# Down products over eight PSUM banks at once, with the second cross attention issued between them

## The reference, cut to what matters

```python
h  = silu(x @ Wgate.T) * (x @ Wup.T)           # 1792 hidden, weights dequantised, with LoRA
x  = layernorm(x + h @ Wdown.T)                # first down stage, then "x2"
s  = x @ (Wq.T @ Wk) @ ctx.T + beta            # second cross attention, per sequence of 128
x  = layernorm(x + softmax(s / sqrt(512)) @ ctx)   # "x3"
h  = silu(x @ G.T * gs) * (x @ U.T * us)       # ternary weights with a scale per row
x  = layernorm(x + (h @ Dn.T) * ds)            # second down stage, the output
```

## Time and profile before

| | us |
|---|---|
| median of 3 runs (721.57 to 722.71) | 722.56 |
| the profiled execution's own time | 721.29 |
| its span in the trace | 719.5 |
| PE busy | 668.8 (93%) |
| DVE busy | 404.9 (56%) |
| ACT busy | 379.6 (53%) |
| POOL busy | 66.9 (9%) |

### The profile page before, as it was taken

How to read it: one execution, slowest core, us unless ns; L and a number is a source line. 1 busy time by engine, 2 the same in 40 slices (tenths; PEclk the granted TensorE clock), 3 DMA queues, 4 the chain that set the end, 5 groups by cost and what they waited for, 6 DMA issues and landing times.

```text
span 719.5 us, 8570 instructions
## 1 busy us (share of the span) xinstructions
PE 668.8 (93%) x3228; PEld 468.4 (65%) x3228; DVE 404.9 (56%) x694; ACT 379.6 (53%) x536; POOL 66.9 (9%) x126
## 2 busy tenths in 40 slices
PE   5789999999998789999999999999997999999992
PEld 3544454545544348787877788888665888887872
DVE  3367768768558786474746434457677222223486
ACT  4456678965556418666666413444335333335653
POOL 1022213201111000000000000001121000000022
PEclk9979999999999899999999999999999999999997
DMA  5682086423223212242423000012641222210002
GB/s 156 204 288 91 2 267 195 153 79 103 70 62 95 89 33 92 63 124 63 123 64 96 1 0 1 0 35 85 246 149 30 61 86 60 88 31 0 1 29 89
DMA packets 24503, 62.97 MB, mean 88 GB/s; under 512 B 5477, under 2 KB 9637, under 8 KB 23566
## 3 DMA queue, kind: packets, MB, share of 16 engines
q1 hardware_dynamic: 24462, 62.43, 27.2%
HBM read 57.68 MB, written 4.73 MB: 87 GB/s over the span
## 4 chain that ended last, share of the span: by engine, by line
PE 81%; DVE 8%; ACT 4%; issue 2%; DMA 2%; POOL 1%; SPq 1%; POOLq 0%; DVEq 0%; ACTq 0%
PE bank L877 16%; PE bank L862 7%; PE bank L864 7%; PE bank L863 7%; PE bank L946 7%; PE bank L947 7%; PE bank L730 4%; PE bank L660 4%; PE bank L510 2%; PE bank L771 2%; PE bank L826 2%; PE bank L758 2%; PE bank L610 2%; PE bank L575 1%; PE bank L586 1%
## 5 line engine op out<-in xcount | busy, mean ns | idle before, releaser
L999 ACT ACTIVATE line<-line 128x1024 f32<-128x1024 f32 x87 | 91.1, 1047 | 0.1
L877 PE MATMUL bank<-wh,xh 128*128 128x512 f32 x224 | 87.8, 392 | 2.0 <-DVE xl L1684 1.8
L946 PE MATMUL bank<-xh,wh 128*128 128x512 f32 x224 | 87.4, 390 | 1.5 <-issue 1.5
L862 PE MATMUL bank<-xh,wh 128*128 128x512 f32 x224 | 88.7, 396 | 0.0
L877 PE MATMUL bank<-wh,xl 128*128 128x512 f32 x224 | 87.4, 390 | 0.0
L864 PE MATMUL bank<-xh,wl 128*128 128x512 f32 x224 | 87.3, 390 | 0.0
L863 PE MATMUL bank<-xl,wh 128*128 128x512 f32 x224 | 87.2, 389 | 0.0
L947 PE MATMUL bank<-xl,wh 128*128 128x512 f32 x224 | 87.2, 389 | 0.0
L1337 POOL TENSOR_SCALAR rstd<-mv 128x1 f32<-128x1 f32 x45 | 20.1, 447 | 633.0 <-DVE mv L1698 467.6
L1227 ACT ACTIVATE xh<-arena 128x512 fp32r<-128x512 f32 x56 | 35.4, 632 | 68.0 <-PE bank L877 59.8
L1684 DVE TENSOR_TENSOR xl<-arena,xh 128x512 fp32r<-128x512 f32 x56 | 38.5, 688 | 52.5 <-ACT xh L1227 52.3
(11 more groups left out here) (175 smaller groups left out, 1176.4 us busy)
## 6 DMA issues: line engine op xcount, KB each, us to landing
codes<-in_c_gu SPq DMA_DIRECT2D x14, 512.0 KB, 4.7
scales<-in_s_gu SPq DMA_DIRECT2D x28, 256.0 KB, 3.9
codes<-in_t_gu SPq DMA_DIRECT2D x14, 512.0 KB, 3.7
codes<-in_c_dn SPq DMA_DIRECT2D x7, 512.0 KB, 4.9
scales<-in_s_dn SPq DMA_DIRECT2D x14, 256.0 KB, 3.9
fold<-in_t_dn SPq DMA_DIRECT2D x1, 3584.0 KB, 12.8
codes<-in_c_qkv SPq DMA_DIRECT2D x6, 512.0 KB, 4.5
arena<-in_xT SPq DMA_DIRECT2D x4, 512.0 KB, 5.0
```

The costliest lines, as they stand in the source:

```text
L862: pe.matmul(dst, wh[:, s, c:c + P], xh[:, k, cols], start=(k == 0), stop=False)
L877: last = pe.matmul(late_bank(b)[:, :], h[:, s, b * P:(b + 1) * P], wp[:, s, 0:D], start=first and p == 0, stop=last_one and p == len(parts ...
L946: pe.matmul(dst, wh[:, s, c:c + P], xh[:, k, cols], start=(k == 0), stop=False)
L999: nc.scalar.activation(below(slot), below(slot), ACT.Prelu, bias=bias, scale=scale, alpha=alpha).then_inc(bent, 1)
```

## The change

Both down stages become one pass over all 8 blocks, with one bank for each block. Tiles 0 to 9 of the first stage (0 to 7 of the second) are walked tile by tile, all 8 blocks each. The last 4 tiles (6 in the second) are then walked block by block, so that blocks end one after another. A tile is prepared once, 1024 tokens wide, in four operand slots instead of two; the second stage puts its tiles 12 and 13 into two more, in the memory of `line` (`late_hidden`), with their weights in `wl`.

Between the block-wise products of the first stage stands the second cross attention: in step n PE issues block n's last 12 products in two groups of 6, with steps of blocks n-1, n-2 and n-3 around them. The x2 norm gets its own statistics tiles (`st2`, `mv2`, `rstd2`) and semaphores, ACT applies both norms (Identity with scale and bias), and DVE adds eps. POOL's stream alternates: the power for x2 of block n, then power and shift for x3 of block n-3. The third feed forward starts with group 0 of tiles 0 and 1 inside steps 8 and 9. The context is loaded when tile 13 has been split, the last down weights (`t_dn`) when its weight has been.

```diff
+TAIL = 3 * NT
+SLOTS = 4
+DN_LAST, T_LAST = NF - 4, NF - 6
...
+        def down_ready(j):
+            return j + 2
...
@@ sync
-                sp.wait_ge(dn_ready, NF + used)
+                sp.wait_ge(dn_low, down_ready(used - 1))
                 sp.dma_start(dst, src).then_inc(done, 16)
-            sp.wait_ge(d_ps, NT)
+            sp.wait_ge(dn_wlow, NF)
             sp.dma_start(t_dn, i["t_dn"]).then_inc(in_tdn, 16)
@@ tensor
+            def dn_group(j):
+                if j:
+                    dn_landed(j)
+                for b in range(NT):
...
+                    last = dn_products(j, b)
+                last.then_inc(hu_used, 1)
+            def dn_block(b, tiles, done=None):
+                for j in tiles:
+                    if b == 0:
+                        dn_landed(j)
+                    last = dn_products(j, b)
+                if done is not None:
                     last.then_inc(done, 1)
+            for j in range(DN_LAST):
+                dn_group(j)
...
+            half = DN_LAST + (NF - DN_LAST) // 2
+            for n in range(NT + 3):
+                if n < NT:
+                    dn_block(n, range(DN_LAST, half))
+                if 2 <= n < NT + 2:
+                    x_probT(n - 2)
+                if n < NT:
+                    dn_block(n, range(half, NF), d_ps)
+                if 1 <= n <= NT:
+                    x2_T(n - 1)
+                if 2 <= n < NT + 2:
+                    x_out(n - 2)
+                if 1 <= n <= NT:
+                    x_scores(n - 1)
+                if n >= 3:
+                    x3_T(n - 3)
+                if n >= NT:
+                    for q in range(n - NT, min(n - NT + 1, 2)):
+                        t_gu_pair(q, 0)
+            for j in range(2):
+                t_gu_pair(j, 1)
...
+            for j in range(T_LAST):
+                t_group(j)
+            for b in range(NT):
+                for j in range(T_LAST, NF):
+                    if b == 0:
+                        t_landed(j)
+                    last = t_products(j, b)
+                last.then_inc(t_d_ps, 1)
@@ scalar
+            for j in range(1, NF):
+                act.wait_ge(h_ready, TG * (j + 1) + 4)
+                if j >= SLOTS:
+                    act.wait_ge(hu_used, j - SLOTS + 1)
+                hidden_hi(hidden_part(xh, j), j, WHOLE, dn_hi)
+                dn_weight_hi(j)
...
+            for n in range(NT + 4):
+                if 2 <= n < NT + 2:
...
+                    nc.scalar.activation(probT[:, b % 2, :], late_bank(b)[:, P:2 * P], ACT.Copy).then_inc(xpT_ready, 1)
+                if 1 <= n <= NT:
+                    x_T_out(n - 1, late_index(n - 1), xT, x2_ps, x2_ready)
+                if n == NT:
+                    act.wait_ge(d_ps, NT)
+                    for s in range(2):
+                        t_gu_cast(s, 0, None)
+                if 3 <= n < NT + 3:
+                    norm_tail(3 * NT + n - 3)
+                if n < NT:
+                    x2_norm(n)
+                if 1 <= n <= NT:
...
+                    nc.scalar.activation(prob[:, b % 2, :], late_bank(b)[:, 0:P], ACT.Exp, bias=x_small(b, 0),
+                                         scale=float(D) ** -0.5, accum_out=x_small(b, 1)).then_inc(x_exp, 1)
+                if 3 <= n < NT + 3:
+                    x_T_out(4 * NT + n - 3, late_index(n - 3), xh)
...
+                if SLOTS <= j < NF - 2:
+                    act.wait_ge(t_used, j - SLOTS + 1)
+                hidden_hi(t_hidden_part(xh, j), j, WHOLE, t_dhi)
+                t_weight(j)
@@ gpsimd
+            def x2_rstd_of(b):
+                pool.wait_ge(x2_stats, b + 1)
+                nc.gpsimd.tensor_tensor(rstd2[:, b % 2, 1:2], rstd2[:, b % 2, 0:1], minus_half[:, :], ALU.pow).then_inc(x2_pow, 1)
+            for n in range(NT + 3):
+                if n < NT:
+                    x2_rstd_of(n)
+                if n >= 3:
+                    rstd_of(3 * NT + n - 3)
@@ vector
+            for n in range(NT + 4):
+                if n < NT:
+                    x2_stats_of(n)
+                if 1 <= n <= NT:
+                    x_max_of(n - 1)
+                if n < NT:
+                    x2_shift(n)
+                if 2 <= n < NT + 2:
+                    x_add(n - 2)
+                    stats_of(3 * NT + n - 2)
+                if 3 <= n < NT + 3:
+                    x_low(4 * NT + n - 3, (n - 3 + 2) % len(bank))
```

More of the change, by code:

```diff
@@ L869, in _ @@
                     gu_tile(s, 2 * n + s)
[L872 to L881, removed]
-                    last.then_inc(done, 1)
@@ L884, in down @@
[L884 to L894, removed]
@@ L896, in _, with down_products, dn_products @@
-            down((dn_ready,), ((xh, wh), (xh, wl), (xl, wh)), hu_used, d_ps, h_ready)
+            def down_products(b, hiddens, weights, first, last):
+                for p, (h, w) in enumerate(zip(hiddens, weights)):
+                    ins = pe.matmul(late_bank(b)[:, :], h[:, b * P:(b + 1) * P], w, start=first and p == 0, stop=last and p == len(hiddens) - 1)
+                return ins
+            def dn_products(j, b):
+                h, l, wh_j, wl_j = hidden_part(xh, j), hidden_part(xl, j), down_part(wh, j), down_part(wl, j)
+                return down_products(b, (h, h, l), (wh_j, wl_j, wh_j), j == 0, j == NF - 1)
@@ L935, in x3_T @@
[L935 to L946, removed]
-                    last = pe.matmul(dst, wh[:, s, c:c + P], xl[:, k, cols], start=False, stop=(k == KD - 1))
-                last.then_inc(done, 1)
@@ new lines, in _, with t_silu @@
+            silu_table()
+            def t_silu(j, tg):
+                s = j % 2
+                act.wait_ge(in_ts[s], 16 * (j // 2 + 1))
+                act.wait_ge(t_gate_ps, t_place(j, tg) + 1)
+                nc.scalar.activation(hT[:, j, tg * 512:(tg + 1) * 512], t_bank(j, tg, 0), ACT.Silu, scale=ff_s[:, s, 0:1]).then_inc(t_sil, 1)
+            for tg in range(TG):
+                for j in range(2):
+                    t_silu(j, tg)
+                    if tg:
+                        t_gu_cast(j, 1, 2 * (j + 1) + 1 - j)
@@ new lines, in _, with t_weight @@
+            for n in range(1, NF // 2 - 1):
+                for s in range(2):
+                    for tg in range(TG):
+                        t_silu(2 * n + s, tg)
+                    t_gu_cast(s, n + 1, 4 * n + 2 * s + 2)
+            def t_weight(j):
+                nc.scalar.activation(t_down_part(j), t_dn[:, j, :], ACT.Copy).then_inc(t_dw, 1)
+            for tg in range(TG):
+                t_silu(NF - 2, tg)
+            t_silu(NF - 1, 0)
+            act.wait_ge(in_tdn, 16)
+            act.wait_ge(t_up_ps, TG * NF - 1)
@@ L1314, in _ @@
+            for m in range(4 * NT, 5 * NT):
                 norm_tail(m)
@@ L1335, in rstd_of @@
                 pool.wait_ge(ln_stats, m + 1)
-                if m not in TURN:
+                if m < 3 * NT and m not in TURN:
                     link(nc.gpsimd.tensor_scalar(rstd[:, m % 2, 0:1], mv[:, m % 2, 1:2], LN_EPS, None, ALU.add))
@@ new lines, in t_hidden @@
+            def t_hidden(j, tg):
+                s = j % 2
+                dve.wait_ge(t_sil, t_place(j, tg) + 1)
+                dve.wait_ge(t_up_ps, t_place(j, tg) + 1)
+                h = hT[:, j, tg * 512:(tg + 1) * 512]
+                nc.vector.scalar_tensor_tensor(h, t_bank(j, tg, 1), ff_s[:, s, 1:2], h, ALU.mult, ALU.mult).then_inc(t_h, 1)
+            for tg in range(TG):
+                for j in range(2):
+                    t_hidden(j, tg)
+            for j in range(2, NF - 1):
+                for tg in range(TG):
+                    t_hidden(j, tg)
```

384 lines of the change are left out of this document (165 added, 219 removed).

## The result

The kernel after the change takes 729.16 us (median of 4 runs, 726.91 to 729.38) against 722.07 us for the kernel before (median of 4, 720.95 to 722.71). The ratio is 1.0093 [1.0068, 1.0117]: slower by 0.9%, with the direction as forecast and inside the range (720.5 to 731), but +7.1 us where +3.2 were forecast, and just above the 723.9 to 729 that the forecast itself covers.

What follows compares the result with a forecast made beforehand. PE's stream, busy 93%, was taken as the bound, only its waits and the tail as savable. Attention +7.9, second down stage +0.8 and tail -5.5 gave +3.2, added to the median: 725.8 us, range 720.5 to 731.

Steps and rivals of the forecast that it cites:

- The ring: Attention loop, steps 3 to 7: chain between blocks' last products through DVE, POOL, ACT, PE takes 7.96 us; PE waits 1.75, +8.8.
- the rival of slow powers: POOL's powers in the attention loop take 1.07 us each, adding 5 us, 731; chance 0.06.
- Start and end of the loop, tile 13: PE waits around the attention loop: 4.4 us at its start, 3.9 at its end, 1.1 for the first down stage's tile 13.
- The rival of smaller waits: Half of the 8.3 us of waits at the loop's start and end is gone: 721.8, no measurable change; chance 0.15.
- The table load: ACT's load ahead of the first exponential costs 1.28 us by the row, not the Trainium skill's 2.66.
- the granted clock: PE's clock in the attention, taken to stay at full speed, 2.4 GHz, at no cost.
- the drop: Rival: the clock falls to 1.2 GHz in the attention, doubling PE's part of five steps, +16, 742; chance 0.02.
- the attention's forecast: Attention beside the first down stage costs 46.1 us against 38.2, waits included: +7.9.
- Second down stage: Old waits go, new ones of 1.2, 1.0 and 1.0 us come at tiles 11 to 13: 54.8 us, +0.8.
- Tail: From PE's end to the span's end one block is left, not four: 7.35 us against 12.8, -5.5.
- Transfers: Context load takes 7.7 us with 5 us of cover; the down weights behind it may slow it; taken as nothing.
- Time against the median: The forecast's +3.2 was added to the median of runs, as the profiled execution's own time was 1.3 under it.

Runs made afterwards that it cites:

- POOL's order alone: The changed kernel with two calls swapped in POOL's loop, power and shift of x3's block n-3 ahead of x2's power: 718.95 us, ratio 0.9962 to the kernel before.
- both orders: The changed kernel with POOL taking x3's block before x2's, and the second down stage's tiles 12 and 13 prepared and used early: 714.39 us, ratio 0.9889.

## Why the prediction was right in direction and short in size

**The ring: right, a little too large.** Forecast were 7.96 us a step and a wait of 1.75, five times. The trace has 7.80 to 7.82 and a wait of 1.57. One pass around it, DVE, POOL and ACT in order of time, from the product that started at 521.13:

```profile
521.56 0.69 DVE L1821 TENSOR_TENSOR x<-x,bank 128x512 f32<-128x512 f32 x1 [1.37 <-PE bank L909]
522.28 0.69 DVE L1823 BATCH_NORM_STATS2 st<-x 128x6 f32<-128x512 f32 x1
523.01 0.18 DVE L1824 BATCH_NORM_AGGREGATE mv<-st 128x2 f32<-128x6 f32 x1
523.23 0.15 DVE L1825 TENSOR_SCALAR rstd<-mv 128x1 f32<-128x1 f32 x1
```

```profile
523.46 0.55 POOL L1442 TENSOR_TENSOR rstd<-rstd,minus_half 128x1 f32<-128x1 f32 x1 [6.38 <-DVE rstd L1825]
523.98 0.55 POOL L1433 TENSOR_TENSOR rstd<-rstd,minus_half 128x1 f32<-128x1 f32 x1
524.62 0.27 POOL L1436 TENSOR_SCALAR rstd<-mv,rstd 128x1 f32<-128x1 f32 x1
```

```profile
524.92 0.81 ACT L1125 ACTIVATE x<-x,rstd 128x512 f32<-128x512 f32 x1 [2.33 <-POOL rstd L1436]
```

Every link of the forecast is there with its length from the earlier trace rows. The 0.16 us too many are mostly POOL's first power, 0.52 to the next one's start where I had 0.62, and PE's overlap at the transposes. Both powers took 0.55, not the 1.07 of the earlier trace rows, so the choice between the two rows was right, and the rival of slow powers falls. My reason for it, that DVE reads PSUM in these steps, was hardly tested: DVE stood still from 523.4 to 524.25, and the rule of the Trainium skill (GPSIMD Engine Reference, Key points) agrees with the short row.

**Start and end of the loop, tile 13: right, in sum a little too large.** Forecast and traced waits in us: tile 13 1.1 and 1.12; x2's first transposes 1.0 and 0.86; first scores 0.9 and 0.69; first softmax transpose 1.9 and 1.66, the second 0.6 and 0.24; the seventh 0.7 and 0.39; the last output 0.5 and 0.37; the first gate product of the last 4 blocks 1.6 and 1.50. At the short waits a traced idle time is up to 0.2 shorter than what the wait costs, as the overlap of two PE instructions is lost with it, so most of these agree; the second and the seventh softmax transpose were taken 0.3 too large. The wait of block 5's x3 for ACT's casts (1.1 forecast) is not in this trace, as PE came late to it, at 558.09, with the lower clock just ahead; in the kernel with POOL's order alone it is there with 0.92. The rival of smaller waits was wrong. The attention with its waits filled costs 45.6 us where the forecast had 46.1.

**The table load.** The trace's 1.28 us was right. The Trainium skill (ScalarE: Activation LUTs, What ACT_TABLE_LOAD costs) gives 2.66 us for a switch, its drain included, and that isn't what it cost here: with the load out of the way the wait before the softmax transpose is 1.4 us shorter, 0.25 of it is left, and the attention is 1.4 us shorter.

**The step that failed: the granted clock.** The forecast put the clock at nothing and rested that on the earlier trace rows, PE busy 28.76 of 33.20 us with the clock at 1.00; the drop got 0.02 and +16. But no single wait of PE in that stretch was longer than 0.7 us, so it couldn't speak for waits of 1.6. Chance and price were both off. The drop came, and it cost 3.7 us in the attention, not 16: it held for a part of two steps, which it made 1.57 us longer each, and behind the fifth wait. The clock came back each time, where the rival had it low throughout. A repeated wait of 1.57 us beside 6.2 of work was enough. The Trainium skill (TensorE: Matmul & The Clock Gate, Part 1) was right in kind: the clock is halved after idle time. With PE's 7.9 us of waits in the loop filled by products the drop was gone. With 3.7 in place of 0, the sum of the attention's forecast, +7.9, is +11.6 where +10.8 was traced. That the measured time still lies inside the range is partly luck: its upper end, 731, was set for slow powers, which did not come, and the clock had been left out of it.

**Second down stage: right in its waits, short by the clock.** Three waits of 1.2, 1.0 and 1.0 were forecast. They are 1.11, 0.73 and 0.36 as idle time, and the products behind the second of them, up to about 701 us, are slower (mean clock 0.93 from 694 to 718). Together the stage is +1.3, not +0.8. In the kernel with the old attention and this stage the same three waits and the clock made it 57.0 us, so the clock's share moves between kernels. Without the waits both are gone.

**Tail: right.** 7.39 us by the trace, 7.35 by the forecast. One block is left, not four. Its norm, in ACT's timeline, 3.6 us ahead of the span's end:

```profile
723.58 0.81 ACT L1125 ACTIVATE x<-x,rstd 128x512 f32<-128x512 f32 x1 [1.90 <-POOL rstd L1436]
```

**Transfers: right.** No wait for the context appears. The down weights behind it on SP's queue took longer (in the list of DMA issues, 16.4 us to landing against 12.8 before):

```profile
fold<-in_t_dn SPq DMA_DIRECT2D x1, 3584.0 KB, 16.4
```

No wait of PE is put down to them.

**Time against the median.** The sum in the profiled execution is 10.8 + 1.3 - 5.4 = +6.7, and the timed difference +7.1. The rest of the span's +7.7 is the untouched start.

## What to carry to other kernels

An in-order engine that serves two chains ties them together: write out which of its instructions waits first, and put the one whose data is already there ahead of the one that must wait for this step's products. Two lines in another order were worth more here than the whole interleaving, which by itself gained nothing measurable, and a reordering of tiles so that those with free buffers come first was worth 4 us. A wait of the busiest engine that comes back each step should be priced twice, once as idle time and once with products at the lower clock behind it. Filling it gives back the second part, removing it both.

## What the runs showed of the hardware that was not expected

- The granted clock of PE fell to its lower level with waits of only 1.57 us, when they came back every 7.8 us with 6.2 us of work between them. It did so in alternate steps: 7.80, 9.38, 7.82, 9.37 us. With waits of 2.20 us three of four steps were long, and the mean of that stretch was 0.87 against 0.91; with the waits filled, or removed by POOL's order alone, it was 1.00. With both orders it was 0.96, as the clock fell there behind one wait of 1.25 us.
- More work made the kernel faster: 30 products that nothing reads took 3.7 us off the attention by the trace (49.3 to 45.6) and 0.57% off the run, with intervals that just touch.
- Not settled: why the lower clock takes every second step and not each one, why the same wait of 1.25 us behind the same instructions was followed by the lower clock in one execution and not in another, and why behind three similar waits (1.11, 0.74 and 0.69 us against 1.11, 0.73 and 0.36) the second down stage took 57.0 us in one kernel and 55.2 in another. The traces give the granted clock, not what decides it.
